# A causal mask on VectorE, and layer norms moved into the FFN before them, in a two-layer kernel

## What is computed

```
x = x + 0.5 * L0_ffn(L)     # 16 routed experts, 4 for each row, and a shared FFN (352)
x = x + L0_attn(L)          # one head: scores from two rank-32 projections, causal softmax, sums of L
x = x + 0.5 * L0_ffn(L)     # the routed FFN once more
x = x + 0.5 * L1_ffn(L)     # silu(L Wg^T * gs) * (L Wu^T * us), then Wd^T * ds, 704 wide
x = x + L1_attn(L)          # 16 heads of 128: rotary q and k, causal softmax, v, Wo
x = x + 0.5 * L1_ffn(L)

q_values = jnp.where(causal, q_values, -jnp.inf)       # the mask, in both attentions
weights = jax.nn.softmax(q_values, axis=-1)
```

## Time and profile before

| | |
|---|---|
| median of 3 runs | 2184.12 us (2183.26 to 2187.24) |
| the profiled execution | 2182.38 us |
| its span | 2180.6 us |
| mean granted TensorE clock | 0.992 of full speed |
| busy share: TensorE, VectorE, ScalarE, GpSimd | 95%, 68%, 61%, 42% |
| first FFN, work of its first dummy matmul to that of the next stage | 466.0 to 591.7 us |
| second attention | 591.7 to about 2058 us |
| second FFN | 2059.5 to 2180.6 us |

### The profile page before, as it was taken

The page is one execution under the profiler, slowest core; times in us unless marked ns, Lnnn a source line. Parts: engine busy times, 40 slices in busy tenths (PEclk is TensorE's granted clock), DMA queues, the critical chain, the costliest instruction groups (busy, mean ns, idle before and its releaser), DMA issues. The chain is left out here.

```text
span 2180.6 us, 41705 instructions
## 1 busy us (share of the span) xinstructions
PE 2068.1 (95%) x14574; PEld 1820.4 (83%) x14574; DVE 1473.0 (68%) x3379; ACT 1339.3 (61%) x3382; POOL 908.1 (42%) x834
## 2 busy tenths in 40 slices
PE   5888978989989999999999999999999999999889
PEld 3665866657869999999999999999999998999778
DVE  6645757645367768777687777777777767777552
ACT  4223642224267777777787777777778768777552
POOL 0342002433243554545445355364454545535232
PEclk9999989999999999999999999999999999999999
DMA  5453042550000000000000000000000000000100
GB/s 203 101 115 54 2 147 58 141 118 1 32 13 6 4 9 11 4 6 9 8 6 9 6 4 13 6 4 6 9 9 6 9 6 9 4 2 1 45 10 30
DMA packets 50990, 67.32 MB, mean 31 GB/s; under 512 B 10080, under 2 KB 36960, under 8 KB 50656
## 3 DMA queue, kind: packets, MB, share of 16 engines
q1 hardware_dynamic: 40416, 51.80, 7.6%
q0 software_dynamic: 10368, 12.85, 3.5%
HBM read 49.15 MB, written 15.48 MB: 30 GB/s over the span
## 5 line engine op out<-in xcount | busy, mean ns | idle before, releaser
L988 ACT ACTIVATE phase_p<-phase_scores,phase_bias 128x512 f32<-128x512 f32 (+3 forms) x680 | 416.3, 626 | 86.4 <-DVE phase_bias L976 86.4
L1033 DVE TENSOR_TENSOR phase_pt_lo<-phase_ring,phase_pt_hi 128x512 fp32r<-128x512 f32 (+3 forms) x680 | 392.7, 605 | 102.7 <-ACT phase_pt_hi L1028 96.7
L969 DVE TENSOR_REDUCE phase_peaks<-phase_scores 128x1 f32<-128x512 f32 (+3 forms) x680 | 398.1, 602 | 59.6 <-PE phase_scores L958 51.9
L1028 ACT ACTIVATE phase_pt_hi<-phase_ring 128x512 fp32r<-128x512 f32 (+3 forms) x680 | 345.2, 534 | 132.8 <-PE phase_ring L1013 128.0
L122 PE MATMUL phase_y<-phase_pt_hi,phase_v_hi 128*128 128x256 f32 (+1 forms) x1152 | 343.2, 298 | 1.6 <-DVE phase_y_lo L1877 1.6
L1013 PE MATMUL phase_ring<-sb_ident,phase_p 128*128 128x128 f32 x2312 | 339.2, 273 | 4.5 <-ACT phase_p L988 2.8
L124 PE MATMUL phase_y<-phase_pt_hi,phase_v_lo 128*128 128x256 f32 (+1 forms) x1152 | 321.5, 279 | 0.0
L123 PE MATMUL phase_y<-phase_pt_lo,phase_v_hi 128*128 128x256 f32 (+1 forms) x1152 | 321.3, 279 | 0.0
L1013 PEld LDWEIGHTS phase_ring<-sb_ident,phase_p 128*128 128x128 f32 x2312 | 261.5, 140 | 26.6 <-ACT phase_p L988 7.3
L1892 POOL TENSOR_TENSOR phase_straight<-phase_rot,phase_rope 64x512 f32<-64x512 f32 x128 | 163.8, 1280 | 279.1 <-ACT phase_rot L1781 279.1
L1909 POOL TENSOR_TENSOR sb_x<-sb_x,phase_part 128x512 f32<-128x512 f32 x128 | 164.8, 1287 | 259.0 <-ACT phase_part L1816 256.5
(11 more groups left out here) (249 smaller groups left out, 4966.5 us busy)
## 6 DMA issues: line engine op xcount, KB each, us to landing
phase_e_up<-expert_up SPq DMA_DIRECT2D x32, 352.0 KB
phase_e_dn<-expert_down SPq DMA_DIRECT2D x32, 256.0 KB
y_rows<-phase_zero SPq DMA_DIRECT2D x8, 512.0 KB, 9.0
xn_rows<-phase_ln_xn SPq DMA_DIRECT2D x8, 512.0 KB, 6.4
sb_x<-y_rows POOLq DMA_DIRECT2D x8, 512.0 KB, 10.8
phase_raw_qk<-qk SPq DMA_DIRECT2D x16, 256.0 KB, 2.5
phase_raw_up<-up SPq DMA_DIRECT2D x10, 256.0 KB, 4.3
sb_x<-x SPq DMA_DIRECT2D x4, 512.0 KB, 7.0
```

The lines of the kernel that those rows point to most:

```text
L969: dve.tensor_reduce(self.peaks[:, t % 2, c:c + 1], self.scores[:, at:at + self.width(t, c)], AX.X, ALU.max).then_inc(*self.peaked.one)
L988: act.activation(self.p[:, at:at + width], self.scores[:, at:at + width], ACT.Exp, bias=self.bias[:, t % 2:t % 2 + 1], accum_out=self.sums ...
L1028: act.activation(hi, value, ACT.Copy).then_inc(*self.t_hi.one)
L1033: dve.tensor_tensor(lo, value, as_f32(hi), ALU.subtract).then_inc(*self.t_lo.one)
```

## The change

The mask: `pe_score` issues no mask matmul. On the diagonal chunk, VectorE adds a row of zeros and the mask (`hide`, of which the last w columns are read) in place to the scores in PSUM and takes their peak with one `tensor_tensor_reduce`.

The norms of the FFNs and of the second attention are made by a new class, `ChunkNorm`, chunk by chunk. The square root and the reciprocal are one power of -0.5 on GpSimd (`pool_power`), and VectorE's small operations are four and not six. In the FFNs the steps stand behind pieces by two tables, `NORM` and `NEXT`. `NEXT` belongs to the first FFN alone: chunks 0 to 2 of its result are normalised and turned for the second attention, which then has only chunk 3 to do. Ahead of chunk 0 the FFNs round the weights of four pieces and not six; the number of dummy matmuls changes; the first FFN loads `rope` and head 0's `qk`, at the end of its own loads, and its down products of chunk 2 run in piece (3, 1).

`Routed` and `Attention0` keep `Norm`.

```diff
+        self.hide = sb("hide", [P, CH], BF16)
+        self.half = sb("half", [P, 4], F32)
+        self.rope, self.raw_qk = sb("rope", [P, T], F32), sb("raw_qk", [P, HK, 2, P], F32)
...
+    def pool_power(self, pool, c):
+        tiles = slice(4 * c, 4 * c + 4)
+        pool.wait_ge(*self.varied[self.tag, c])
+        pool.tensor_tensor(self.rstd[:, tiles], self.var[:, tiles], self.core.half[:], ALU.pow).then_inc(*self.powered.one)
+    def dve_inverse(self, dve, c):
+        tag, tiles = self.tag, slice(4 * c, 4 * c + 4)
+        var, rstd, tmp = (a[:, tiles] for a in (self.var, self.rstd, self.tmp))
+        dve.wait_ge(*self.powered[tag, c])
+        dve.tensor_tensor(tmp, rstd, rstd, ALU.mult).then_inc(*self.step.one)
+        dve.wait_ge(*self.step[tag, c, 0])
+        dve.scalar_tensor_tensor(tmp, tmp, -0.5, var, ALU.mult, ALU.mult).then_inc(*self.step.one)
+        dve.wait_ge(*self.step[tag, c, 1])
+        dve.scalar_tensor_tensor(rstd, tmp, 1.5, rstd, ALU.add, ALU.mult).then_inc(*self.step.one)
+        dve.wait_ge(*self.step[tag, c, 2])
+        if self.by_act:
+            dve.scalar_tensor_tensor(self.shift[:, tiles], self.mv[:, tiles, 0], -1.0, rstd, ALU.mult, ALU.mult).then_inc(*self.step.one)
...
         h, t, c = key
-        diag, at = c == t // 4, self.bank(key) * BANK
-        n = max(256, self.width(t, c))
+        at, n = self.bank(key) * BANK, max(256, self.width(t, c))
         if old := self.old_chunk[key]:
             pe.wait_ge(*self.p_done[old])
         for k, (a, b) in enumerate(pairs(n)):
             done = pe.matmul(self.scores[:, at:at + n], a, b, start=k == 0, stop=k == len(pairs(n)) - 1)
-        if diag:
-            at += t % 4 * P
-            done = pe.matmul(self.scores[:, at:at + P], self.core.ident_b[:], self.core.mask_b[:], start=False, stop=True,
-                             skip_group_check=True)
         done.then_inc(*self.scored.one)
     def dve_peak_of_chunk(self, dve, key):
         h, t, c = key
         at = self.bank(key) * BANK
         dve.wait_ge(*self.scored[key])
-        dve.tensor_reduce(self.peaks[:, t % 2, c:c + 1], self.scores[:, at:at + self.width(t, c)], AX.X, ALU.max).then_inc(*self.peaked.one)
+        w = self.width(t, c)
+        scores, peak = self.scores[:, at:at + w], self.peaks[:, t % 2, c:c + 1]
+        if c == t // 4:
+            dve.tensor_tensor_reduce(scores, scores, self.core.hide[:, CH - w:], 1.0, NEG, ALU.add, ALU.max, peak).then_inc(*self.peaked.one)
+        else:
+            dve.tensor_reduce(peak, scores, AX.X, ALU.max).then_inc(*self.peaked.one)
...
+    NORM = {(0, 1): [("scale", 0, 1)], (0, 3): [("turn", 0, 1)], (0, 4): [("measure", 0, 2)], (1, 0): [("scale", 0, 2)],
+            (1, 2): [("turn", 0, 2)], (1, 3): [("measure", 0, 3)], (2, 0): [("scale", 0, 3)], (2, 2): [("turn", 0, 3)]}
+    NEXT = {(1, 4): [("measure", 1, 0)], (1, 5): [("scale", 1, 0)], (2, 1): [("turn", 1, 0)], (2, 3): [("measure", 1, 1)],
+            (2, 5): [("scale", 1, 1)], (3, 0): [("turn", 1, 1)], (3, 2): [("measure", 1, 2)], (3, 4): [("scale", 1, 2)],
+            (3, 5): [("turn", 1, 2)]}
...
+            self.norms.append(ChunkNorm(core, sb, then, range(NCH - 1), after=lambda c: self.added[tag, c, 3], like=self.norm))
...
-        return I1M - 1 if c == NCH - 1 else 1
+        return I1M - 1 if c == NCH - 1 and not self.then else 1
...
+        if self.then:
+            sp.dma_start(core.raw_qk[:], src["qk"][0]).then_inc(*core.loads("attn1_in_qk").one)
+            sp.dma_start(core.rope[:], src["rope"]).then_inc(*core.loads("rope_in").one)
...
-        self.core.keep_warm(pe, self.down_ps[:, 0, :], 55 if self.add_y else 25)
-        self.norm.pe_turn(pe, (0,))
-        self.core.keep_warm(pe, self.down_ps[:, 0, :], 5)
+        bank = self.down_ps[:, 0, :]
+        self.core.keep_warm(pe, bank, 55 if self.add_y else 14)
+        self.pe_turn(pe, 0, 0)
+        self.core.keep_warm(pe, bank, 5)
         for c in range(NCH):
             for m in range(I1M):
-                if c == 0 and m == 2:
-                    self.core.keep_warm(pe, self.down_ps[:, 0, :], 10 if self.add_y else 4)
                 self.pe_up(pe, c, m)
                 if c and m == self.down_after(c):
                     self.pe_down(pe, c - 1)
-                if m == 2 and c + 1 < NCH:
-                    self.norm.pe_turn(pe, (c + 1,))
+                for what, n, chunk in self.behind[c, m]:
+                    if what == "turn":
+                        self.pe_turn(pe, n, chunk)
         self.pe_down(pe, NCH - 1)
...
-        tag, norm = self.tag, self.norm
-        norm.act_root(act, 0)
-        norm.act_rows(act, 0)
+        tag = self.tag
+        self.norm.act_rows(act, 0)
         self.act_up_weights(act, 0)
-        norm.act_turn(act, (0,))
-        self.act_up_weights(act, 1)
-        norm.act_root(act, 1)
-        for m in range(2, I1M):
+        self.act_turn(act, 0, 0)
+        for m in range(1, 4):
             self.act_up_weights(act, m)
-        norm.act_rows(act, 1)
         act.wait_ge(*self.scales_in[tag, 2])
         for c in range(NCH):
             for m in range(I1M):
                 self.act_piece(act, c, m)
-                if m == 5 and c == 0:
-                    for g in (2, 3):
-                        norm.act_root(act, g)
-                if m == 0 and 0 < c < NCH - 1:
-                    norm.act_rows(act, c + 1)
+                if c == 0 and m == 0:
+                    for late in range(4, I1M):
+                        self.act_up_weights(act, late)
                 if m == 2 and c == 0:
                     act.wait_ge(*self.scaled[tag])
                     act.activation(self.dn_hi[:], self.raw_dn[:], ACT.Copy).then_inc(*self.down_w_hi.one)
-                if m == 2 and c + 1 < NCH:
-                    norm.act_turn(act, (c + 1,))
+                for what, n, chunk in self.behind[c, m]:
+                    if what == "scale":
+                        self.norms[n].act_rows(act, chunk)
+                    elif what == "turn":
+                        self.act_turn(act, n, chunk)
...
+                for what, n, chunk in self.behind[c, m]:
+                    if what == "measure":
+                        self.norms[n].dve_stats(dve, chunk)
+                    elif what == "scale":
+                        self.norms[n].dve_inverse(dve, chunk)
+                        self.norms[n].dve_rows(dve, chunk)
+                    elif what == "turn":
+                        self.dve_turn(dve, n, chunk)
...
+        for c in range(2):
+            self.norm.pool_power(pool, c)
         for m in range(2, I1M):
...
+                    if what == "measure":
+                        pool.wait_ge(*idle)
+                        self.norms[n].pool_power(pool, chunk)
+                        idle = self.norms[n].powered[self.norms[n].tag, chunk]
...
-        order = [("load_qk", 0), ("load_wv", 0), ("project", 0, 0), ("finish", 0, 0), ("project", 0, 1),
-                 ("score", 0, 0, 0), ("peak", 0, 0), ("exp", 0, 0)]
+        order = [("stats", NCH - 1), ("load_qk", 0), ("project", 0, 0), ("scale", NCH - 1), ("finish", 0, 0), ("project", 0, 1),
+                 ("flip", NCH - 1, 0), ("flip", NCH - 1, 1), ("load_wv", 0), ("score", 0, 0, 0), ("peak", 0, 0), ("exp", 0, 0)]
...
-        core.keep_warm(pe, self.y[:], 46)
-        self.norm.pe_turn(pe, (0, 1))
-        core.keep_warm(pe, self.y[:], 14)
-        self.norm.pe_turn(pe, (2, 3))
-        core.keep_warm(pe, self.y[:], 5)
-        pe.wait_ge(*self.norm.ready)
+        core.keep_warm(pe, self.y[:], 6)
         for step in self.order:
             what, key = step[0], step[1:]
             if step == ("score", 0, 0, 0):
-                core.keep_warm(pe, self.y[:], 20)
-            if what == "project":
+                core.keep_warm(pe, self.y[:], 6)
+            if what == "flip":
+                self.norm.pe_flip(pe, *key, self.flip_bank(key[1]))
+            elif what == "project":
                 h, g = key
                 bank, where = self.both(step), slice(2 * P * g, 2 * P * (g + 1))
                 if g == 0:
                     pe.wait_ge(*self.w_lo["qk"][h,])
+                if h == 0:
+                    self.norm.wait_turned(pe, g // 2)
...
-        for g in range(2):
-            self.norm.act_root(act, g)
-        loads = [step for step in self.order if step[0].startswith("load")]
-        for step in loads[:2]:
-            self.act_weights(act, step)
-        for g in range(2):
-            self.norm.act_group(act, g)
...
+            if what == "stats":
+                pool.wait_ge(*idle)
+                self.norm.pool_power(pool, *key)
+                idle = self.norm.powered[self.tag, key[0]]
```

190 lines of the change are left out of this document (156 added, 34 removed).

## The result

The changed kernel takes 2159.94 us (median of 4 runs, 2159.06 to 2163.37) against 2184.6: a ratio of 0.9881, 95% interval 0.9868 to 0.9894. It is faster, by 25 us where 44 were forecast. The profiled execution took 2159.53 us.

A forecast was written before the change was run, and what follows sets the result against it. TensorE's own instruction stream was taken to bound the second attention. Terms -16 - 1 (masks), -14 (second attention's head), -1.8 and -11.0 (FFNs) sum to -43.8 us, forecasting 2140 us, range 2124 to 2161.

The forecast's parts named there:

- (a): Rival, masks: gain absorbed by more TensorE waits, or the new instruction costs near +0.4 us; 2152 us, chance 0.15.
- (b): Rival, seams between stages give less: power a microsecond dearer, or three half-clock stretches; 2148 us, chance 0.12.
- Price of the mask: Second attention: removing mask matmuls saves 0.07 us before each transpose and 0.13 before each product, 22.3 us.
- I keep 16 of 22.3 us: Second attention: of TensorE's saving some 6 us is given back in waits on other engines' chains; bounds 0 and 22.
- nothing at 0.1: Second attention: a VectorE instruction 0.1 us longer costs TensorE nothing, with rooms before transposes spread evenly from 0.15 to 1.84 us.
- Head of the second attention: Stage start to first score: 13.0 us in place of 29.4, less copies and half clock; -14 us, bounds -9 and -17.
- First FFN: Whole stage: 8.7 us saved in chunk 0, against added turns, a new tail wait and half clock; -1.8 us, bounds +4 and -8.
- The stall is gone: First FFN, chunk 0: with the gate right behind the first piece, TensorE's wait for act at the third piece vanishes; 4.5 us.
- Net 3.5: First FFN, tail: new wait for the last piece's h_lo before the last down products, 4.4 us less the last turn.
- Second FFN: Whole stage: fewer dummies 2.3 us, third piece reached earlier 4.5, and 1.6 and 2.6; -11.0 us, bounds -5 and -13.
- (c): Rival, second attention: combined mask instruction so slow that peak, bias and exponential set the pace; 2202 us at X = 1.1, chance 0.04.
- (d): Rival: the mask's matmuls cost nothing because each hides in the drain of the scores; 2157 us, chance 0.03.

The follow-up runs named there:

- e3: Kernel before with the mask part of the change alone, plus padding so every later tensor lies 2,048 bytes further; 2171.99 us, ratio 0.9946.
- e7: Kernel of e3 with the plain peak reduction on the diagonal too, so no mask is computed at all; 2169.55 us, ratio 0.992.
- e12: Changed kernel with the tail of e8 and 1,248 bytes of padding, shifting tensors by whole multiples of 2048; 2153.26 us, ratio 0.986.
- e8: Kernel of e6 with second and third chunks' norm steps earlier in the first FFN and 12 dummy matmuls behind the last turn; 2154.63 us, ratio 0.9851.
- e6: Kernel of e5 with 32-byte fillers so that every tensor of a stage begins at a multiple of 64 bytes; 2158.45 us, ratio 0.9874.
- e11: Kernel before with each mask matmul issued twice; 2196.96 us against 2184.42, ratio 1.0059.
- e5: Changed kernel with an unused tensor of 32 bytes a partition behind half; 2159.6 us, ratio 0.9878.
- e1: Kernel before with one unused tensor of 784 bytes a partition behind the small constants; 2190.38 us against 2183.5, ratio 1.0028.

## Why the prediction was right and wrong

Direction and mechanism stood: TensorE's stream bounds the second attention, and normalising three chunks earlier takes 14 us from its head. The time, 2160, lies within the range by 1 us, and above both of the rivals (a) and (b). It is what the two give together (2140 + 12 + 8), but it came about otherwise, so its place in the range is in part luck: the range was drawn for one rival at a time. By its steps:

- **Price of the mask.** 22.3 us forecast, 19 to 21 seen (e3, and the changed kernel). Right.
- **"I keep 16 of 22.3 us".** The step that failed in the second attention. In e3 11 were kept. The waits that I put at "some 6 us" were 7.7, of which 3.3 to 4.4 are the combined instruction's. Its price was 0.067 us, under my 0.1; what failed is "nothing at 0.1", an average over rooms taken as even from 0.15 us up. The tightest places recur from head to head (e7), and there even 0.067 us shows in full. The changed kernel kept 10, of which 1.2 are the new head's. The shifted tensors slowed the products that read `xt`, a term that the sum did not have: e12, with the pitches of before, kept 12.8. So the sign "two heads shorter by 2 us" failed: they were shorter by 1.1.
- **Head of the second attention.** -14 forecast, -14.2 seen. The first score came 15.2 us behind the stage's start and not 13.0: the power cost 1.01 and not 0.5 us, and the chain from projection to score took 10.65 and not 8.9, with VectorE's rows slowed beside GpSimd and about 5 us at a granted clock of 0.50. The total stands because I had set 2.6 us aside, 1.6 of them for copies ahead of the first exponential, which are no part of the way to the first score. The fallen clock was among the signs of being wrong; the term stayed within its bounds.
- **First FFN.** -1.8 forecast with +4 as its bound; +8.4 seen. Three steps failed. "The stall is gone": it was, and five others of the same sum came, since I asked only whether piece 2 would find its `act`, and not what the down weights and chunk 1's rows, queued between the gates, do to the pieces behind. Of 8.7 us, 4.1 were kept. "Net 3.5" of the tail: the last piece's chain was right (e8: 4.3 us), but the scale step stood ahead of it, which I had not placed in ScalarE's and VectorE's queues; with the half clock behind it this cost 2.6 us (e8 beside e6). And "nothing" for the added turns' surroundings: waits of 0.71 and 1.32 us at the second chunk's down products and at the turn behind piece (3, 0); e8 took the second away.
- **Second FFN.** -11.0 forecast, -6.5 seen, within its bounds. The dummies gave 1.8 of 2.3; chunk 0 gave 5.5 of 8.7, with waits of 0.70, 0.36 and 1.90 us at the same places as in the first FFN; the pitch of the up products took 0.8 back.
- **Other rivals.** (c): the instruction was 0.067 us dearer, far from 1.0. (d): e3 and e11 speak against it. A one-time load of code at the first power: it took 1.05 us at 474.50 and 1.01 later, so no row shows one. The Trainium skill's 6 us for a first call (GPSIMD Engine Reference, section "Instruction dispatch") did not come for this instruction.

What stays open: which relation between the places of two operands slows a product. Shifts of 0, 2,048 and 12,288 bytes were fast and 800, 11,040 and 12,320 slow in the FFNs, but the kernel of e5 (11,072 in the FFNs, slow; 832 for the projections, fast) separates the two, and no single remainder that I tried explains both. And what part of the remaining 4 us of waits belongs to which chain.

## What to carry to other kernels

Work that leaves the bounding engine's stream is kept only until it meets the next engine's chain: here 19 us of matmuls gave 11, while adding such matmuls cost nearly all of their pitch. When a table moves small steps behind pieces, write out each engine's queue for the piece in which they stand; a step in front of the next gate holds TensorE, and at the last piece of the first FFN the clock fell with it (2.6 us together). After any change in the allocation, compare the pitch of unchanged products first: a shift alone was worth 6 us here.

## What the runs showed of the hardware

- The place of operands in SBUF changes a matmul's pitch: 0.227 to 0.233 us for 512 columns and 0.117 to 0.120 for 256, with the same instructions; 784 unused bytes made the kernel 0.28% slower (e1).
- An add with a running maximum in place over PSUM is a pass (690 ns at 512 wide, 292 at 128) and a read of 138 ns that starts about 84 ns before the pass's end: 748 ns together at 512 wide, 348 at 128, which is 67 more than the plain maximum takes.
- Operations of VectorE on four elements a partition took 0.15 and 0.16 us alone, 1.20 and 1.21 beside a GpSimd subtraction; two rows of 256 took 0.73 us, and 2.81 beside two GpSimd operations.
- A power of four elements a partition takes GpSimd 1.01 us, nearly what a 512-wide subtraction takes there (1.28).
- After 2.46 us of idle time the granted clock fell from 1.00 to 0.50, stayed there for 6.7 us, through a turn and the first down products, and rose to 1.00 again; the 72 down products took 10.60 us and not 8.79. Where the turn followed at once and 12 dummy matmuls stood behind it, it stayed at 1.00 (e8).
